# A two-number scaling step of the softmax moved from ScalarE to VectorE, in a kernel whose order a planner lays out

## The chip, the cores and the metric

The kernel runs on one core of a Trainium2 chip. The metric is the device time of one execution, in microseconds, and of several executions the median. A profile is one execution recorded by the hardware profiler. The engines are TensorE (PE; its weight loads are PEld), VectorE (DVE), ScalarE (ACT), GpSimd (POOL) and SyncE (SP), which only issues DMAs here.

## The reference

The input is 16 batches of 512 rows of 512 numbers, f32. Each row is layer-normed once, and the result goes through attention and through a gated feed-forward layer side by side; both results are added to the input.

```python
xn = layernorm(x)                                   # x: 16 x 512 x 512
qkv = xn @ w_qkv.T + b_qkv                          # 16 heads of 32
scores = q @ k.T / sqrt(32) + causal                # 512 x 512 for each head
attn = softmax(scores) @ v
a = attn @ w_out.T + b_out
g = xn @ gate_w.T * gate_s;  u = xn @ up_w.T * up_s # 1408 wide, weights -1, 0, 1
f = (silu(g) * u) @ down_w.T * down_s
out = x + a + f
```

## The kernel before

**Number format.** Values are kept as pairs of f16 (a high part and the rest), so each projection is two or three f16 matmul passes. ScalarE writes the high part, VectorE subtracts it from the f32 value and writes the rest. That is so for the scores' probabilities too (steps `ph` and `pl` below).

**Work.** A batch takes 456 matmuls of 512 columns in the projections (lines 805, 812, 821, 830 and 838), 64 for the scores (line 892) and 192 small ones for attention times values (line 906). TensorE's results go to four PSUM banks `psW`, the scores to four others, `psS`.

**Softmax.** A batch has four groups `G` of four heads. The unit `u` is one head and one block of 128 query rows, so a group has 16 units and the kernel 1024; a unit with block `i` has 128(i+1) keys. Units are joined in 10 cells a group (a block of 512 or the pair 128 and 384 or two of 256, which fills a PSUM bank), so there are 640 cells, 384 of two units and 256 of one. A cell goes through these steps:

- `sn` (PE, line 892): the scores, one matmul a unit, into the cell's `psS` bank
- `max` (DVE, line 1151): adds the mask, finds the row's extreme
- `exp` (ACT, line 1288): exponential in place, with its row sum into `rsum`
- `rc` (DVE, line 1157): `rinv = 1 / rsum`, one instruction for the cell's one or two columns
- `rc2` (ACT, line 1294): `rinv = rinv * 2**14`, in place, one instruction for the cell
- `ph` (ACT, line 1307): `exp * rinv` as f16 into `PL` (or `PL3b`)
- `pl` (DVE, line 1162): the rest as f16
- `pt` (a DMA transpose, line 754): from `PL` to `PT`, when the four heads of a block are done; then `pv` (PE, line 906), `oh` (ACT, 1318), `ol` (DVE, 1166) and the output projection (PE, 821)

A bank of `psS` is free for the next `sn` after the `pl` of the cell four before it.

**Order.** Every engine runs a fixed list of steps. A class `Plan` makes the lists when the kernel is built: it plays the kernel with an assumed duration of each step (`TIMES`) and an assumed delay until another step can use a result (`HOP`, 120 ns for DVE, 130 ns for ACT), and at each moment it gives an engine that is free the ready step with the earliest due time. The due times follow the units, 1795 ns each (`UNIT`); the softmax of the first 160 units is due up to 25 us later (`LATE`), so that it catches up afterwards. At run time the lists are fixed: an engine that has come to a step waits for it, whatever else is ready. A step waits on semaphores that count the finished steps of one kind.

The planner counts `rc` as 100 ns of DVE and `rc2` as 200 ns of ACT, and gives both the same due time:

```python
self.chain(due + 1500, "dve", ("rc", u), ("act", "exp", u))
self.chain(due + 1500, "act", ("rc2", u), ("dve", "rc", u))
```

GpSimd normalises the rows (`nrm`, line 1366), splits them (`xl`, 1375), writes the rest of the hidden values (`hl`, 1383) and adds up the output (`ya` and `yb`, 1388 and 1393). It and VectorE's `tensor_scalar` appear in a list `SHARED` of steps that the planner doesn't let overlap; it names `ffw` (line 1092, VectorE converting the feed-forward weights at the start) but neither `rc` nor `rc2`.

Of the kernel before, what the change touches and what calls it, by code (L numbers as in the profile page):

```python
# [38 lines left out]
    "stats": 605, "aggr": 85, "nrm": 2080, "nrm0": 500, "spread_bv": 1000, "qk_part": 720, "qk_max": 450, "qk_scales": 2100, "qk_small": 650, "wqk_lo": (270, 600),  # L39
    "v_part": 720, "v_max": 100, "v_scales": 1500, "wv_lo": 670, "o_part": 720, "o_max": 100, "o_scales": 1700, "wo_lo": 670, "mid": 550, "xTl": 670, "xTh": 600,  # L40
# [52 lines left out]
class Plan:  # L93
# [254 lines left out]
    def scores(self, u):  # L348
        G = u // 16
        due = AT + UNIT * u - LEAD + self.late(u)  # L350
        c = cell(u)
        units = cell_units(c)
        free = [("dve", "pl", cell_units(c - NS)[-1])] if c >= NS else []
        self.chain(due, "pe", ("sn", u), ("sp", "pk", G), *free)
        self.chain(due + 400, "dve", ("max", u), ("pe", "sn", units[-1]), ("pool", "mask"))
        self.chain(due + 1000, "act", ("exp", u), ("dve", "max", units[-1]))
        if u != units[-1]:
            return
        self.chain(due + 1500, "dve", ("rc", u), ("act", "exp", u))
        self.chain(due + 1500, "act", ("rc2", u), ("dve", "rc", u))  # L360
        for v in units:
            i, h = ORDER[v % 16]
            before = G - 2 if i == 3 else G - 1
            free = [("sp", "pt", before, i)] if before >= 0 else [("pe", "chk", i ^ 1)] * (i >= 2) if G == 0 else [PE_BIAS, ("pe", "chk", 4)]
            self.chain(due + 2000, "act", ("ph", v), ("act", "rc2", u), *free)
        for v in units:
            i, h = ORDER[v % 16]
            self.chain(due + 2600, "dve", ("pl", v), ("act", "ph", u))
            if h == 3:
                free = [("pe", "pv", G - 1)] if G else [("pe", "chk", 12), *(("dve", "wqk_lo", s, 1, 3) for s in range(2)), ("dve", "wv_lo", 1)]  # L370
                self.chain(due + 3000, "sp", ("pt", G, i), ("dve", "pl", v), *free)
# [157 lines left out]
def block_kernel(nc, x, w_qkvT, b_qkv, w_outT, b_out, gateT, upT, downT, gate_s, up_s, down_s, out):  # L529
# [121 lines left out]
    def done(engine, *step):  # L651
        return at[engine, *step]
# [25 lines left out]
    with nc.Block() as block:  # L678
# [278 lines left out]
        def _(e):  # L957
# [41 lines left out]
            for step, *k in plan.order["dve"]:  # L999
# [100 lines left out]
                elif step == "flag2":  # L1100
                    dve.wait_ge(*done("pe", "red", "flag", 1))
                    dve.wait_ge(*done("dve", "ff_scales"))
                    dve.wait_ge(*done("sp", "scale_d"))
                    land(e.tensor_copy(flaga, tile(("red", "flag"))[:, 128:131]))
                    land(e.tensor_scalar(flaga[:, 1:3], flaga[:, 1:3], 0.5, None, op0=ALU.is_lt))
                    e.tensor_reduce(bada, flaga, axis=AX.X, op=ALU.max).then_inc(sem["dve flag2"], 1)
                    dve.wait_ge(*done("dve", "flag2"))
                    land(e.tensor_scalar(okf, bada, 0.0, None, op0=ALU.is_equal))
                    land(e.tensor_tensor(okf, okf, hs[:, 1:2], op=ALU.mult))
                    land(e.tensor_scalar(scale_d[:, :], scale_d[:, :], okf, None, op0=ALU.mult))  # L1110
                elif step == "ql":
                    b, g, which = k
                    bias = bqs[:, 4 * which + g:4 * which + g + 1]
                    dve.wait_ge(*done("act", "qh", b, g, which))
                    e.scalar_tensor_tensor(stg[:, 2 * which + 1, :], tile(("qk", *k))[:, :], bias, stg[:, 2 * which, :], op0=ALU.add, op1=ALU.subtract).then_inc(  # L1115
                        sem["dve ql"], 1)
                elif step == "vl":
                    b, t = k
                    dve.wait_ge(*done("act", "vh", b, t))
                    e.tensor_tensor(V[:, t, 1, :], tile(("v", *k))[:, :], V[:, t, 0, :], op=ALU.subtract).then_inc(sem["dve vl"], 1)  # L1120
                elif step == "yf":
                    b, t = k
                    dve.wait_ge(*done("pe", "o", b, t))
                    dve.wait_ge(*done("pool", "ya", 4 * b + t))
                    e.scalar_tensor_tensor(y[t][:, :], tile(("o", *k))[:, :], s_out, y[t][:, :], op0=ALU.mult, op1=ALU.add).then_inc(sem["dve yf"], 1)
                elif step == "yt":
                    b, t = k
                    dve.wait_ge(*done("pe", "dn", b, t))
                    if b or t:
                        dve.wait_ge(*done("pool", "ya", 4 * b + t - 1))  # L1130
                    else:
                        dve.wait_ge(*done("dve", "flag2"))
                        dve.wait_ge(*done("act", "o_part", 3))
                    e.tensor_tensor(y_t, tile(("dn", *k))[:, :], scale_d[:, :], op=ALU.mult).then_inc(sem["dve yt"], 1)
                elif step == "gate":
                    A = act_t[plan.gu_units[tuple(k)] % 3][:, :]
                    dve.wait_ge(*done("act", "th", *k))
                    e.scalar_tensor_tensor(A, A, 1.0, tile(("ga", *k))[:, :], op0=ALU.add, op1=ALU.mult).then_inc(sem["dve gate"], 1)  # L1138
                elif step == "up":
                    m = k[1]  # L1140
                    A = act_t[plan.gu_units[tuple(k)] % 3][:, :]
                    dve.wait_ge(*done("pe", "up", *k))
                    dve.wait_ge(*done("dve", "gate", *k))
                    dve.wait_ge(*done("dve", "ff_scales"))
                    e.scalar_tensor_tensor(A, tile(("up", *k))[:, :], gus[:, m:m + 1], A, op0=ALU.mult, op1=ALU.mult).then_inc(sem["dve up"], 1)  # L1145
                elif step == "max":
                    u = n
                    s = s_tile(u)
                    dve.wait_ge(*done("pe", "sn", cell_units(cell(u))[-1]))
                    dve.wait_ge(*done("pool", "mask"))  # L1150
                    e.tensor_tensor_reduce(s, s, mask[:, 512 - s.shape[1]:512], scale=negsc, scalar=BIG, op0=ALU.add, op1=ALU.min,  # L1151
                                           accum_out=nmax[:, u % 16:u % 16 + 1]).then_inc(sem["dve max"], 1)
                elif step == "rc":
                    units = cell_units(cell(n))
                    part = slice(units[0] % 16, n % 16 + 1)
                    dve.wait_ge(*done("act", "exp", n))
                    e.reciprocal(rinv[:, part], rsum[:, part]).then_inc(sem["dve rc"], 1)  # L1157
                elif step == "pl":
                    i, h = ORDER[n % 16]
                    out = PLv[pl_tile(n // 16, i)]  # L1160
                    dve.wait_ge(*done("act", "ph", cell_units(cell(n))[-1]))
                    e.scalar_tensor_tensor(out[:, :, 2 * h + 1, :], p_blocks(n), rinv[:, n % 16:n % 16 + 1], out[:, :, 2 * h, :],  # L1162
                                           op0=ALU.mult, op1=ALU.subtract).then_inc(sem["dve pl"], 1)
                elif step == "ol":
                    dve.wait_ge(*done("act", "oh", n))
                    e.scalar_tensor_tensor(oT[:, n % 5, 1, :], tile(("pv", n))[:, :], 2.0 ** -14, oT[:, n % 5, 0, :], op0=ALU.mult, op1=ALU.subtract).then_inc(  # L1166
                        sem["dve ol"], 1)
                else:
                    raise ValueError(step)
# [36 lines left out]
        def _(e):  # L1206
# [9 lines left out]
            for step, *k in plan.order["act"]:  # L1216
# [67 lines left out]
                elif step == "exp":  # L1284
# [2 lines left out]
                    act.wait_ge(*done("dve", "max", cell_units(cell(u))[-1]))  # L1287
                    e.activation(s, s, ACT.Exp, bias=nmax[:, u % 16:u % 16 + 1], scale=-1.0,  # L1288
                                 accum_out=rsum[:, u % 16:u % 16 + 1]).then_inc(sem["act exp"], 1)
                elif step == "rc2":  # L1290
                    units = cell_units(cell(n))
                    part = slice(units[0] % 16, n % 16 + 1)
                    act.wait_ge(*done("dve", "rc", n))
                    e.activation(rinv[:, part], rinv[:, part], ACT.Copy, scale=2.0 ** 14).then_inc(sem["act rc2"], 1)  # L1294
                elif step == "ph":
                    i, h = ORDER[n % 16]
                    before = n // 16 - (2 if i == 3 else 1)
                    act.wait_ge(*done("act", "rc2", cell_units(cell(n))[-1]))
                    if before >= 0:
                        act.wait_ge(*done("sp", "pt", before, i))  # L1300
                    elif n // 16 == 1:
# [140 lines left out]
```

## Time and profile before

| | |
|---|---|
| Time, median of 3 (lowest, highest) | 1911.43 us (1909.62, 1912.43) |
| The profiled execution | 1912.43 us |
| Its span, first to last instruction | 1910.7 us |
| PE busy | 1867.6 us (98%) |
| DVE busy | 1616.4 us (85%) |
| ACT busy | 1471.1 us (77%) |
| POOL busy | 647.7 us (34%) |
| Mean granted TensorE clock | 0.996 |

The span is read from the trace, and 1.7 us of the execution lie around it. A matmul is shown until its result is out, and the next begins before that, so a busy PE is one that isn't seen standing still.

### The profile page before, as it was taken

The page shows a single profiled execution, that of the slowest core. Times are in us where ns is not written, and L with a number is a line of the kernel's source. Part 1 is how long each engine was busy: PE and PEld are TensorE (multiplying, and loading weights), DVE is VectorE, ACT ScalarE, POOL GpSimd, SP SyncE. Part 2 cuts the span into 40 slices and gives each one's busy share as a digit, 9 for nine tenths or more (in the row PEclk, how much of TensorE's full clock was granted, in tenths as well). Part 3 has the DMA queues.
Part 4 walks back from the last instruction along what each step waited for, and adds up shares of the span by engine and source line. Part 5 has one row for each costly group of instructions (what it writes and reads, how often), then busy time and mean ns, then how long its engine had stood idle before and what let it go on. Part 6 is the DMA issues. An engine that isn't in the chain of part 4 may idle for free.

```text
span 1910.7 us, 35064 instructions
## 1 busy us (share of the span) xinstructions
PE 1867.6 (98%) x11560; PEld 879.1 (46%) x11560; DVE 1616.4 (85%) x4697; ACT 1471.1 (77%) x4441; POOL 647.7 (34%) x593
## 2 busy tenths in 40 slices
PE   7899999999999999999999999999999999999997
PEld 3444444444444444444444444444444444444443
DVE  7998999888788888889888788888888888788882
ACT  5678888877787777878877787777878778787771
POOL 1863262342423424233242423424233232312121
PEclk9999999999999999999999999999999999999998
DMA  8399999898988899798997988899798997987893
GB/s 271 82 188 183 173 197 153 162 173 148 163 142 147 153 178 157 143 170 129 173 175 133 172 138 154 156 171 154 151 161 137 178 168 136 156 133 140 131 171 78
DMA packets 805114, 299.90 MB, mean 157 GB/s; under 512 B 734145, under 2 KB 766913, under 8 KB 804929
## 3 DMA queue, kind: packets, MB, share of 16 engines
q1 hardware_dynamic: 804928, 297.62, 88.0%
q8 instruction: 93, 1.52, 0.4%
q14 instruction: 93, 0.75, 0.1%
HBM read 46.94 MB, written 16.78 MB: 33 GB/s over the span
## 4 chain that ended last, share of the span: by engine, by line
PE 79%; DMA 5%; DVE 5%; SPq 4%; POOL 3%; ACT 3%; issue 1%; POOLq 0%; ACTq 0%; DVEq 0%
PE psW L830 28%; PE psW L805 15%; PE psW L838 9%; PE psW L812 8%; PE psW L821 8%; PE psS L892 7%; PE psW L906 5%; DMA PT<-PL 2%; DMA xin<-in_x 2%; SPq L754 2%; DVE PL L1162 1%; SPq L684 1%; DVE psS L1151 1%; POOL xin L1366 1%; ACT PL L1307 1%
## 5 line engine op out<-in xcount | busy, mean ns | idle before, releaser
L830 PE MATMUL psW<-xT,Wgu 128*128 128x512 f16 x2816 | 670.8, 379 | 5.8 <-DVE PT L1115 3.6
L1288 ACT ACTIVATE psS<-psS,small 128x512 f32<-128x512 f32 (+3 forms) x1024 | 516.6, 507 | 163.6 <-DVE small L1151 159.4
L1151 DVE CUSTOM_DVE_ANT_0 psS<-psS,mask,small 128x512 f32<-128x512 f32 (+3 forms) x1024 | 534.5, 551 | 30.3 <-PE psS L892 26.8
L1162 DVE SCALAR_TENSOR_TENSOR PL<-psS,small,PL 128x256 f16<-128x256 f32 (+3 forms) x896 | 424.3, 515 | 54.6 <-ACT PL L1307 53.6
L1383 POOL TENSOR_TENSOR hdn<-act_t,hdn 128x512 f16<-128x512 f32 x176 | 204.3, 1162 | 735.5 <-ACT hdn L1283 735.5
L1307 ACT ACTIVATE PL<-psS,small 128x256 f16<-128x256 f32 (+3 forms) x896 | 400.8, 511 | 19.7 <-DMA PT<-PL 17.5
L830 PEld LDWEIGHTS psW<-xT,Wgu 128*128 128x128 f16 x2816 | 269.8, 97 | 303.0 <-DVE PT L1115 4.1
L805 PE MATMUL psW<-xT,Wqkv 128*128 128x512 f16 x1536 | 363.3, 380 | 0.2 <-DVE act_t L1138 0.2
L838 PE MATMUL psW<-Wdn,hdn 128*128 128x512 f16 x1408 | 316.3, 379 | 0.0
L892 PE MATMUL psS<-QK 96*128 96x512 f16 (+3 forms) x1024 | 252.6, 300 | 12.6 <-DVE PL L1162 10.4
L805 PEld LDWEIGHTS psW<-xT,Wqkv 128*128 128x128 f16 x1536 | 146.1, 98 | 163.2 <-issue 2.2
L1288 ACT ACTIVATION_READ_ACCUMULATOR psS<-psS,small 128x1 f32 x1024 | 217.2, 212 | 0.0
L838 PEld LDWEIGHTS psW<-Wdn,hdn 128*128 128x128 f16 x1408 | 136.7, 98 | 158.7 <-POOL hdn L1383 0.2
L821 PE MATMUL psW<-Wo,oT 128*128 128x512 f16 x768 | 186.9, 382 | 1.5 <-DVE oT L1166 1.5
L812 PE MATMUL psW<-Wqkv,xT 128*128 128x512 f16 x768 | 184.7, 382 | 3.2 <-DVE Wqkv L997 3.2
L1294 ACT ACTIVATE small<-small 128x2 f32<-128x2 f32 (+1 forms) x640 | 124.6, 210 | 52.4 <-DVE small L1157 50.9
L892 PEld LDWEIGHTS psS<-QK 96*128 96x128 f16 x1024 | 95.0, 98 | 142.8 <-DVE PL L1162 41.3
L1283 ACT ACTIVATE hdn<-act_t 128x512 f16<-128x512 f32 x176 | 111.8, 636 | 51.7 <-DVE act_t L1145 51.6
L1275 ACT ACTIVATE act_t<-psW,small 128x512 f32<-128x512 f32 x176 | 121.2, 689 | 32.0 <-PE psW L830 30.2
L1151 DVE DVE_READ_ACCUMULATOR2_ANT small<- 128x1 f32 x1024 | 145.3, 142 | 0.0
L1145 DVE SCALAR_TENSOR_TENSOR act_t<-psW,small,act_t 128x512 f32<-128x512 f32 x176 | 131.2, 745 | 9.5 <-PE psW L830 8.9
L1157 DVE RECIPROCAL small<-small 128x2 f32<-128x2 f32 (+1 forms) x640 | 96.7, 157 | 46.9 <-ACT psS L1288 46.0
(151 smaller groups left out, 1740.6 us busy)
## 6 DMA issues: line engine op xcount, KB each, us to landing
QK<-PT SPq DMA_DIRECT2D x192, 256.0 KB, 5.8
y<-in_x SPq DMA_DIRECT2D x68, 256.0 KB, 3.2
out<-y SPq DMA_DIRECT2D x64, 256.0 KB, 3.5
xin<-in_x SPq DMA_DIRECT2D x60, 256.0 KB, 3.6
PT<-PL SPq DMA_TRANSPOSE x224, 5.1
PT<-in_w_qkvT SPq DMA_DIRECT2D x4, 512.0 KB, 7.1
y<-in_downT SPq DMA_DIRECT2D x4, 256.0 KB, 11.3
xT<-in_w_outT SPq DMA_DIRECT2D x4, 256.0 KB, 3.5
```

The source lines that it names most:

```text
L805: mm = e.matmul(ps[:, :], Wqkv[wl][:, c, c0:c0 + 128], xT[b % 2][:, 4 * xl + c, :], start=(k == 0), stop=last)
L812: mm = e.matmul(ps[:, :], xT[b % 2][:, 4 * xl + c, 128 * t:128 * (t + 1)], Wqkv[wl][:, c, 1024:1536], start=(k == 0), stop=last)
L821: mm = e.matmul(ps[:, :], oT[:, (4 * b + g) % 5, xl, 128 * t:128 * (t + 1)], Wout[wl][:, g, :], start=(k == 0), stop=last)
L830: mm = e.matmul(ps[:, :], Wgu[:, up, c, 128 * m:128 * (m + 1)], xT[b % 2][:, 4 * xl + c, :], start=(k == 0), stop=last)
L838: mm = e.matmul(ps[:, :], hdn[:, m, xl, 128 * t:128 * (t + 1)], Wdn[:, m, :], start=(k == 0), stop=last)
L892: e.matmul(s_tile(u), q[0:96, h, 0, 128 * i:n], q[0:96, h, 1, 0:n], start=True, stop=True).then_inc(sem["pe sn"], 1)
L1145: e.scalar_tensor_tensor(A, tile(("up", *k))[:, :], gus[:, m:m + 1], A, op0=ALU.mult, op1=ALU.mult).then_inc(sem["dve up"], 1)
L1151: e.tensor_tensor_reduce(s, s, mask[:, 512 - s.shape[1]:512], scale=negsc, scalar=BIG, op0=ALU.add, op1=ALU.min, accum_out=nmax[:, u % 16: ...
L1162: e.scalar_tensor_tensor(out[:, :, 2 * h + 1, :], p_blocks(n), rinv[:, n % 16:n % 16 + 1], out[:, :, 2 * h, :], op0=ALU.mult, op1=ALU.subt ...
L1288: e.activation(s, s, ACT.Exp, bias=nmax[:, u % 16:u % 16 + 1], scale=-1.0, accum_out=rsum[:, u % 16:u % 16 + 1]).then_inc(sem["act exp"], 1)
L1307: e.activation(PLv[pl_tile(n // 16, i)][:, :, 2 * h, :], p_blocks(n), ACT.Copy, scale=rinv[:, n % 16:n % 16 + 1]).then_inc(sem["act ph"], 1)
L1383: e.tensor_tensor(hdn[:, m, 1, :], act_t[plan.gu_units[tuple(k)] % 3][:, :], hdn[:, m, 0, :], op=ALU.subtract).then_inc(sem["pool hl"], 1)
```

## The change

The step `rc2` goes from ScalarE's list to VectorE's. There it is a `tensor_scalar` with a constant, in place on the same one or two columns; it waits for `rc`, and `ph` waits for it. The planner gets new durations for both steps, 85 ns each instead of 100 and 200, so it lays out all lists anew.

```diff
-    ... "rc": 100, "rc2": 200, ...
+    ... "rc": 85, "rc2": 85, ...
@@ scores
         self.chain(due + 1500, "dve", ("rc", u), ("act", "exp", u))
-        self.chain(due + 1500, "act", ("rc2", u), ("dve", "rc", u))
+        self.chain(due + 1500, "dve", ("rc2", u), ("dve", "rc", u))
...
-            self.chain(due + 2000, "act", ("ph", v), ("act", "rc2", u), *free)
+            self.chain(due + 2000, "act", ("ph", v), ("dve", "rc2", u), *free)
@@ vector
+                elif step == "rc2":
+                    units = cell_units(cell(n))
+                    part = slice(units[0] % 16, n % 16 + 1)
+                    dve.wait_ge(*done("dve", "rc", n))
+                    e.tensor_scalar(rinv[:, part], rinv[:, part], 2.0 ** 14, None, op0=ALU.mult).then_inc(sem["dve rc2"], 1)
@@ scalar
-                elif step == "rc2":
-                    units = cell_units(cell(n))
-                    part = slice(units[0] % 16, n % 16 + 1)
-                    act.wait_ge(*done("dve", "rc", n))
-                    e.activation(rinv[:, part], rinv[:, part], ACT.Copy, scale=2.0 ** 14).then_inc(sem["act rc2"], 1)
                 elif step == "ph":
...
-                    act.wait_ge(*done("act", "rc2", cell_units(cell(n))[-1]))
+                    act.wait_ge(*done("dve", "rc2", cell_units(cell(n))[-1]))
```

## Rows read from the trace of the kernel before

**Rows 1.** Busy time of each engine by stretch (us, and instructions).

```profile
core 0: us, PE busy (x) PEld busy (x) DVE busy (x) ACT busy (x) POOL busy (x), PEclk, DMA share, GB/s
0.00:60.00 60.00, 44.99 (x197) 21.26 (x198) 48.72 (x123) 32.72 (x79) 20.06 (x32) 0.97 0.72 237
60.00:100.00 40.00, 34.23 (x240) 18.79 (x238) 36.71 (x81) 25.69 (x68) 34.97 (x26) 1.00 0.43 82
100.00:215.00 115.00, 108.38 (x675) 50.00 (x674) 104.84 (x327) 98.09 (x300) 52.82 (x50) 0.99 1.07 180
215.00:330.00 115.00, 114.77 (x756) 54.05 (x754) 106.98 (x330) 99.76 (x312) 46.57 (x44) 1.00 1.00 177
330.00:675.00 345.00, 342.51 (x2126) 160.38 (x2124) 293.33 (x860) 272.81 (x826) 118.82 (x109) 1.00 0.90 156
...
675.00:1710.00 1035.00, 1034.01 (x6412) 487.02 (x6411) 882.03 (x2571) 813.63 (x2465) 333.58 (x301) 1.00 0.91 155
1710.00:1870.00 160.00, 159.17 (x968) 74.70 (x967) 135.62 (x399) 125.50 (x388) 37.11 (x31) 1.00 0.82 144
1870.00:1911.00 41.00, 29.57 (x199) 12.92 (x196) 8.20 (x14) 2.93 (x9) 3.80 (x3) 0.88 0.42 91
```

**Rows 2.** Waits in total, the two small steps and `sn` (us, times, longest).

```profile
ACT small L1294 <- DVE small L1157: 50.9, 97, 2.8
...
PEld psS L892 <- DVE PL L1162: 41.3, 104, 2.8
...
PE psS L892 <- DVE PL L1162: 10.4, 14, 2.5
```

**Rows 3.** The step `rc` (L1157) alone, by stretch: busy, and how many.

```profile
60.00:100.00 40.00, 0.91 (x6) 1.00 0.43 82
100.00:215.00 115.00, 6.93 (x45) 0.99 1.07 180
215.00:330.00 115.00, 6.92 (x46) 1.00 1.00 177
790.00:905.00 115.00, 6.04 (x40) 1.00 0.89 157
```

**Rows 4.** Timeline of VectorE from 25.4 us, one small step behind another.

```profile
25.70 0.17 DVE L973 TENSOR_SCALAR small<-small 128x2 f32<-128x2 f32 x1
25.90 0.16 DVE L1040 TENSOR_TENSOR small<-small 128x2 f32<-128x2 f32 x1
26.09 0.17 DVE L985 TENSOR_SCALAR small<-small 128x2 f32<-128x2 f32 x1
26.30 0.17 DVE L986 RECIPROCAL small<-small 128x2 f32<-128x2 f32 x1
```

**Rows 5.** Timelines of VectorE and of ScalarE from 908 us.

```profile
908.10 0.17 DVE L1157 RECIPROCAL small<-small 128x2 f32<-128x2 f32 x1
908.18 0.74 DVE L1151 CUSTOM_DVE_ANT_0 psS<-psS,mask,small 128x512 f32<-128x512 f32 x1
...
908.96 0.20 ACT L1294 ACTIVATE small<-small 128x2 f32<-128x2 f32 x1
909.05 0.65 ACT L1288 ACTIVATE psS<-psS,small 128x512 f32<-128x512 f32 x1
```

**Rows 6.** Timeline from 112 us, GpSimd and VectorE's `tensor_scalar`.

```profile
112.02 4.15 POOL L1366 TENSOR_SCALAR xin<-xin,small 128x512 f32<-128x512 f32 x2
...
114.77 0.17 DVE L1105 TENSOR_SCALAR small<-small 128x2 f32<-128x2 f32 x1
...
115.55 0.90 DVE L1110 TENSOR_SCALAR scale_d<-scale_d,small 128x512 f32<-128x512 f32 x1
```

**Rows 7.** Timeline from 1870 us, the last cell and the end.

```profile
1871.17 0.16 DVE L1157 RECIPROCAL small<-small 128x2 f32<-128x2 f32 x1
1871.36 0.21 ACT L1294 ACTIVATE small<-small 128x2 f32<-128x2 f32 x1 [0.67 <-DVE small L1157]
1871.60 0.84 ACT L1307 ACTIVATE PL<-psS,small 128x384 f16<-128x384 f32 x2
...
1888.33 3.39 PE L906 MATMUL psW<-PT,V 128*32 128x512 f16 x48 [4.80 <-DMA PT<-PL]
```

2 rows, old and new, of the table TIMES are left out of this document.

## The prediction

> **What bounds the kernel now.** I read the busy time by stretch first, then the waits, then timelines of the places where the two small steps stand.
>
> TensorE is the bound. From 675 to 1710 us it is busy 1034.0 of 1035 us, at full clock, while DVE is busy 882.0 (85%) and ACT 813.6 (79%) [rows 1]. Nothing that makes DVE or ACT a little faster or slower there can be seen in the end, as long as both stay below TensorE and no result comes later than TensorE's list asks for it. TensorE stands still visibly in few places, read as stretch minus busy in [rows 1]: 15.0 us before 60 us (loads and weight scales, before softmax is of any size), 5.8 from 60 to 100, 6.6 from 100 to 215, 0.2 from 215 to 330, 2.5 from 330 to 675, 1.0 to 1710, 0.8 to 1870, and 11.4 in the tail.
>
> The second thing to see is that DVE is nearly full early on. The softmax starts late and catches up: `rc` is run 45 and 46 times in the two stretches of 115 us from 100 to 330 us, against 40 in such a stretch later [rows 3]. DVE is busy 104.8 and 107.0 of 115 us in them, ACT 98.1 and 99.8 [rows 1]. So the change moves work from the second fullest to the fullest of the two helpers, just where there is least room.
>
> The third is how softmax stops TensorE: `sn` waits for the `pl` that frees its bank, 10.4 us in all on the matmul, and 41.3 us on its weight load, most of which lies under the matmul before it [rows 2]. So the latency of a cell counts a little.
>
> **What comes off ACT.** 640 instructions. In a stream, the instruction behind `rc2` begins 0.09 us after it (908.96 to 909.05 in [rows 5]), so 640 x 0.09 = 58 us of ACT's time come free, and up to 640 x 0.20 = 128 us where nothing is behind it (0.20 us is its own duration). ACT also stood idle 50.9 us ahead of `rc2`, waiting for `rc` [rows 2]; that wait passes to `ph`, which now waits for DVE in the same way. All of it lies beside TensorE's work: 0 us.
>
> **What goes onto DVE.** The trace has a `tensor_scalar` of 128x2 f32 on the same small tile: 0.17 us [rows 4]. If another instruction stands between it and `rc`, it costs what `rc` costs in a stream: the next begins 0.08 us later (908.10 to 908.18, [rows 5]). If it stands right behind `rc` and waits for its result, the pair is like the chain of dependent small steps in [rows 4], which begin 0.19 to 0.21 us apart, so `rc2` adds 0.20 us. Hence 640 x 0.08 = 51 us to 640 x 0.20 = 128 us more DVE in all. By stage:
>
> - 675 to 1710 us: nine stretches of 40 cells, 360 x 0.08 to 0.20 = 29 to 72 us on 882, so 911 to 954 of 1035. It fits under TensorE, with at least 81 us to spare: 0 us.
> - 100 to 330 us: 91 cells, 7 to 18 us on 211.8, so 219 to 230 of 230. It fits barely, or only just not.
> - 60 to 100 us has 6 cells, about 1 us more in 3.3 us idle.
>
> **Latency of a cell.** The shortest way from `rc` to `ph` is to be seen at the last cell: `rc` begins at 1871.17, `rc2` at 1871.36, `ph` at 1871.60, so 0.43 us [rows 7]. After the change it is 0.20 (to `rc2`, rows 4) + 0.17 (its duration) + 0.03 (the hop to the other engine, taken from the end of `rc` at 1871.33 to 1871.36, [rows 7]) = 0.40 us. Where ACT is occupied, the difference is larger: at 908 us `rc` began at 908.10 and `rc2` only at 908.96, since ACT was at work on an `exp` [rows 5]. On DVE it would have come after 0.20 us, or behind the `max` that followed, about 0.7 us. So a busy cell wins 0.1 to 0.6 us. What is queued behind the new instruction on DVE (`max`, `pl`, and the evacuations of `psW`, for which TensorE waits) loses 0.08 to 0.20 us for each. I take the two as equal: between 100 and 330 us, where both matter, the cells' gain makes the banks free sooner and the load makes DVE later.
>
> A rule of the Trainium skill speaks against this change, and is weighed here because rows bear on it. The row first: a `tensor_scalar` of 512 columns begun at 115.55 took 0.90 us, ending 0.28 us after GpSimd's instruction, which ran until 116.17; the one of 2 columns, begun at 114.77 while the same GpSimd work was running, took 0.17 us as it does elsewhere [rows 4, 6]. The Trainium skill (SBUF — State Buffer, "Who interferes with whom") says that a VectorE instruction in a mode with two ports and a GpSimd instruction exclude one another for the whole instruction; and VectorE: DVE Perf Modes ("What auto-detection actually checks") has the mode taken by an SBUF-to-SBUF `tensor_scalar` with an even count, which `rc2` is in 384 of 640 cases. The long instruction agrees with it, the short one doesn't. By the row the term is 0; by the rule it is the fourth case below.
>
> **The rest of the plan.** The lists are laid out anew on all engines, with ACT counted 200 ns less a cell and DVE 85 + 85 - 100 = 70 ns more. That shuffles the order everywhere. Its price can't be read; its bounds can. No order can win more than the idle time of TensorE that softmax can touch: 6.6 + 0.2 + 2.5 + 1.0 + 0.8 us from 100 to 1870 us and the 4.8 us for which the last `pv` waits for transposes [rows 7], 15.9 us in all. For the loss, the nearest row is the stretch from 330 to 675: 2.5 us in 345 instead of 1.0 in 1035, which over the 1035 us would be 7.5 - 1.0 = 6.5 us more. I take 0, since both counted durations are near the measured steps (0.085 beside 0.08, and 0.085 + 0.120 for the pair beside 0.20).
>
> **The tail.** After the last `ph` come transposes, `pv`, and the output projection; none changes. The last cells have 0.43 against 0.40 us: 0 us within what can be read.
>
> **Sum.** 1912.4 (the profiled execution; its span 1910.7 + 1.7) + 0 (ACT) + 0 (DVE under TensorE) + 0 (start, two terms against one another) + 0 (order) = 1912.4 us. That execution was the slowest of three; the median is 1.0 us less, so I forecast 1911.4, say 1911.
>
> **The rivals.**
>
> 1. *Nothing to be seen* (forecast): TensorE's load stays the bound, DVE's additional work goes into its idle time. For: 99.9% busy from 675 to 1710 us. Against: the start has little room. 1911 us.
> 2. *Faster through shorter cells.* ACT, relieved of a step, starts `exp` and `ph` sooner, banks come free sooner, and TensorE's stops at `sn` shrink. For: 97 waits of ACT at `rc2`, and 10.4 us of stops at `sn` [rows 2]. Against: the wait only moves to `ph`. Half of the 15.9 us: 1903 to 1904 us.
> 3. *Slower: DVE becomes the bound during the catch-up.* Place: 100 to 330 us. DVE's 18.2 us idle there are waits for results that don't vanish when more work is put in, so its work stretches the stage by what is added, 7 to 18 us; TensorE can fill part of it with feed-forward work, so I take the lower end. It decides from the point where DVE's additional work there exceeds what its idle time absorbs, that is, if most `rc2` stand right behind their `rc` (0.20, not 0.08). 1911 + 7 = 1918 us.
> 4. *Slower through GpSimd.* If `rc2` waited for GpSimd after all: GpSimd is busy 33% of the time (333.6 of 1035), one of its instructions lasts some 1.2 to 2.1 us, so a step meets one in a third of cases and waits about 0.6 us, 0.2 us on the mean. In the catch-up 91 x (0.20 + 0.20) = 36 us on 18 idle, at least 18 us late: 1930 us. Against it stands the row of 0.17 us.
> 5. *The step doesn't get cheaper in latency*: the planner, which lets 120 ns pass after `rc`, fits a long DVE instruction (0.75 us) between the two each time. Then cells are as long as before, DVE pays only 0.08, and the time is that of case 1.
>
> **How the numbers follow.** Chances: case 1 with 5, 0.44; case 2, 0.29; case 3 with an unlucky order, 0.23; case 4, 0.04. Changes under 0.2% (3.8 us) can't be told from none. Faster 0.29, same 0.44, slower 0.27. The range goes to the middle of case 2 and past case 3, 1903 to 1921, and leaves out a better order than half of the idle time, and case 4. Case 1 alone is 1908 to 1915.
>
> **What would show it.** L1294 gone from ACT, 640 `tensor_scalar` of 0.15 to 0.17 us on DVE; one of 0.5 us or more is case 4. DVE busy 50 to 128 us more, ACT 60 to 128 less. PE busy from 675 to 1710 us as before. PE's idle time from 100 to 330 us: 6.8 us now, less in case 2, above 12 in case 3. In case 2 the waits of `sn` for `pl` fall below 10.4 us. The prediction is wrong if TensorE's stops, spread in the middle of the run, turn out to depend on the order laid out anew more than on any engine's load.

## The result and the profile after

The changed kernel takes 1930.9 us (median of 4, 1929.1 to 1932.7) against 1910.9 us before (4, 1909.6 to 1912.4): a ratio of 1.0102, 95% interval 1.0087 to 1.0117. It is 20 us slower. The forecast was 1911 us and no change; the measured time lies outside the range as well.

The profiled execution has a span of 1930.4 us. First the busy time of each engine by stretch, as in [rows 1]:

```profile
0.00:60.00 60.00, 42.99 (x178) 19.86 (x179) 47.95 (x125) 31.26 (x73) 18.81 (x31) 0.91 0.72 237
60.00:100.00 40.00, 34.76 (x246) 19.16 (x245) 36.99 (x84) 24.40 (x61) 33.25 (x26) 1.00 0.39 78
100.00:215.00 115.00, 102.05 (x634) 46.12 (x633) 110.79 (x353) 88.92 (x244) 50.26 (x46) 0.97 0.97 169
215.00:330.00 115.00, 114.12 (x712) 53.46 (x711) 107.49 (x355) 90.47 (x250) 43.01 (x40) 1.00 1.00 177
330.00:675.00 345.00, 340.93 (x2114) 158.81 (x2113) 309.78 (x980) 256.76 (x699) 123.95 (x115) 1.00 0.90 158
675.00:1710.00 1035.00, 1029.26 (x6382) 482.75 (x6380) 921.45 (x2914) 766.91 (x2097) 335.03 (x302) 1.00 0.90 154
1710.00:1870.00 160.00, 158.94 (x1004) 74.24 (x1003) 140.71 (x448) 117.69 (x325) 31.38 (x27) 1.00 0.78 136
```

ScalarE (ACT) has less to do and VectorE (DVE) more, as the change says. From 100 to 215 us DVE is busy 110.8 of 115 us and TensorE stands still 13.0 us instead of 6.6; from 675 to 1710 us TensorE stands still 5.7 us instead of 1.0. The new instruction by its two widths (busy, mean ns of one), among the groups of instructions:

```profile
L1162 DVE TENSOR_SCALAR small<-small 128x2 f32<-128x2 f32 x384 | 99.1, 259 | 4.2
L1162 DVE TENSOR_SCALAR small<-small 128x1 f32<-128x1 f32 x256 | 36.6, 147 | 3.4
```

With one column it takes what was forecast, 0.15 us. With two it takes 0.26 us on the mean, not 0.17. Two places in the timeline show why:

```profile
351.39 2.08 POOL L1366 TENSOR_SCALAR xin<-xin,small 128x512 f32<-128x512 f32 x1
351.55 0.62 DVE L1162 TENSOR_SCALAR small<-small 128x2 f32<-128x2 f32 x1
...
1146.62 1.16 POOL L1383 TENSOR_TENSOR hdn<-act_t,hdn 128x512 f16<-128x512 f32 x1 [8.49 <-ACT hdn L1288]
1146.77 1.09 DVE L1162 TENSOR_SCALAR small<-small 128x2 f32<-128x2 f32 x2
...
1147.84 1.42 ACT L1307 ACTIVATE PL<-psS,small 128x384 f16<-128x384 f32 x3 [0.63 <-DVE small L1162]
```

At 1146.62 us GpSimd begins a step of 1.16 us; `rc2` begins 0.15 us later on DVE and is over only when GpSimd is (the row joins it with the next one), and ScalarE stands idle 0.63 us for it. Counted over the trace, 74 of the 384 two-column `rc2` last over 0.25 us, all of them begun during a GpSimd instruction. Of these, 63 end 21 to 26 ns after that instruction, and the other 11 at the same point within it, 0.78 us after its start, as in the first two rows. None of the 256 one-column ones is long, though 79 begin during GpSimd's work. What the two-column ones take above 0.16 us adds up to 38 us.

Where the time went can be read from the last matmul of the down projection (line 838) of the second, the ninth and the last batch. The last start in each stretch stands behind the "to", before and then after:

```profile
L838 PE MATMUL psW<-Wdn,hdn x176: 377/379/389, 113.7 to 281.7; 128*128 128x512 f16 x176
L838 PE MATMUL psW<-Wdn,hdn x792: 377/379/389, 113.7 to 1089.8; 128*128 128x512 f16 x198
L838 PE MATMUL psW<-Wdn,hdn x1408: 377/379/390, 113.7 to 1883.1; 128*128 128x512 f16 x176
```

```profile
L838 PE MATMUL psW<-Wdn,hdn x176: 376/379/382, 116.3 to 293.5; 128*128 128x512 f16 x176
L838 PE MATMUL psW<-Wdn,hdn x792: 376/379/382, 116.3 to 1104.3; 128*128 128x512 f16 x198
L838 PE MATMUL psW<-Wdn,hdn x1408: 376/379/390, 116.3 to 1905.5; 128*128 128x512 f16 x176
```

So 11.8 us are lost by the end of the second batch, 2.7 in the next seven, 7.9 in the last seven, and the tail after it is 2.7 us shorter (24.9 us instead of 27.6; the granted clock in it is 0.93 instead of 0.81).

### The profile page after: what moved, and what is told of

Read it like the earlier page. It is cut to its first block, busy times and chain, and to the rows that moved or that the text cites. A ratio compares the mean times of both kernels' runs of the same rounds, so it can differ in the third digit from the quotient of the medians.

```text
span 1930.4 us, 35063 instructions
## 1 busy us (share of the span) xinstructions
PE 1872.0 (97%) x11560; PEld 876.3 (45%) x11560; DVE 1705.7 (88%) x5337; ACT 1397.9 (72%) x3801; POOL 647.4 (34%) x593
## 4 chain that ended last, share of the span: by engine, by line
PE 63%; DVE 17%; DMA 8%; SPq 4%; ACT 3%; issue 3%; POOL 2%; ACTq 0%; POOLq 0%; DVEq 0%
PE psW L830 21%; PE psW L805 13%; PE psW L812 8%; PE psW L821 7%; PE psW L838 6%; PE psS L892 5%; DVE PL L1167 4%; PE psW L906 4%; DVE psS L1151 4%; DMA PT<-PL 4%; DMA xin<-in_x 3%; SPq L754 2%; ACT PL L1307 1%; DVE act_t L1145 1%; DVE PL3b L1167 1%
## 5 line engine op out<-in xcount | busy, mean ns | idle before, releaser
L1167 DVE SCALAR_TENSOR_TENSOR PL<-psS,small,PL 128x256 f16<-128x256 f32 (+3 forms) x896 | 418.7, 513 | 55.2 <-ACT PL L1307 54.4
L1307 ACT ACTIVATE PL<-psS,small 128x256 f16<-128x256 f32 (+3 forms) x896 | 394.8, 512 | 74.5 <-DVE small L1162 45.1
L1293 ACT ACTIVATION_READ_ACCUMULATOR psS<-psS,small 128x1 f32 x1024 | 221.1, 216 | 0.0
L1162 DVE TENSOR_SCALAR small<-small 128x2 f32<-128x2 f32 (+1 forms) x640 | 134.1, 214 | 7.7
L1138 DVE SCALAR_TENSOR_TENSOR act_t<-act_t,psW 128x512 f32<-128x512 f32 x176 | 119.4, 679 | 15.6 <-ACT act_t L1280 15.6
```

Source lines behind the costliest of these rows:

```text
L1307: e.activation(PLv[pl_tile(n // 16, i)][:, :, 2 * h, :], p_blocks(n), ACT.Copy, scale=rinv[:, n % 16:n % 16 + 1]).then_inc(sem["act ph"], 1)
```

## The experiments

Three theories stood at the start. **L**: GpSimd holds the two-column `rc2`. **D**: the load that `rc2` puts on VectorE costs the time. **O**, later **S**: the lists that the planner lays out anew are worse, whatever is in them. In the table "lists" says whose order the engines run; the last columns are the start of the last down matmul of batch 2 and of batch 16 in the profile (281.7 and 1883.1 before). The medians come from several chips, so the ratio, to the kernel before on the same chip, is what compares. A profile is one execution: those of e9 and e10 took 1917.7 and 1927.2 us, some 5 us more than their medians, so their last two columns are late by a part of that.

| run | lists | rc2 | median us | ratio (95%) | batch 2 | batch 16 |
|---|---|---|---|---|---|---|
| after | new | DVE | 1930.9 | 1.0102 (1.0087-1.0117) | 293.5 | 1905.5 |
| e1 | new | DVE, one column | 1926.5 | 1.0083 (1.0064-1.0102) | 289.4 | 1897.6 |
| e13 | new | left out | 1920.7 | 1.0059 (1.0042-1.0076) | 286.8 | 1893.3 |
| e12 | before | left out | 1909.6 | 1.0000 (0.9991-1.0010) | 281.6 | 1882.7 |
| e4 | before | ACT, spare on DVE | 1913.2 | 1.0017 (1.0007-1.0027) | 283.0 | 1886.5 |
| e3 | before | ACT, wide spare | 1934.3 | 1.0125 (1.0100-1.0149) | 288.2 | 1907.7 |
| e14 | before | DVE, apart from rc | 1925.4 | 1.0089 (1.0073-1.0106) | 283.2 | 1895.5 |
| e6 | before | DVE, one column | 1942.1 | 1.0165 (1.0147-1.0183) | 292.5 | 1913.1 |
| e5 | before | DVE | 1969.7 | 1.0307 (1.0283-1.0331) | 295.4 | 1940.5 |
| e15 | before | ACT, waiting spare | 1969.5 | 1.0317 (1.0300-1.0334) | 299.7 | 1942.1 |
| e8 | rc 95, rc2 200 | ACT | 1910.9 | 1.0005 (0.9995-1.0014) | 282.1 | 1884.4 |
| e9 | rc 100, rc2 150 | ACT | 1913.0 | 1.0016 (1.0005-1.0028) | 284.5 | 1889.4 |
| e2 | rc 85, rc2 85 | ACT | 1922.4 | 1.0066 (1.0047-1.0086) | 289.7 | 1894.7 |
| e10 | rc 80, rc2 80 | DVE, one column | 1921.8 | 1.0063 (1.0047-1.0080) | 288.7 | 1897.5 |
| e7 | rc 100, rc2 200 | DVE | 1934.7 | 1.0126 (1.0106-1.0146) | 307.7 | 1914.4 |

**e1: GpSimd can't hold it, the changed kernel's lists.**

```diff
-e.tensor_scalar(rinv[:, part], rinv[:, part], 2.0 ** 14, None, op0=ALU.mult).then_inc(sem["dve rc2"], 1)
+for c in range(part.start, part.stop):
+    ins = e.tensor_scalar(rinv[:, c:c + 1], rinv[:, c:c + 1], 2.0 ** 14, None, op0=ALU.mult)
+ins.then_inc(sem["dve rc2"], 1)
```

> The changed kernel with the same order on every engine; only, where rc2 covers two columns it is two tensor_scalar of one column each. In the changed kernel 74 of the 384 two-column rc2 last 0.66 us on the mean and none of the 256 one-column ones is long. Theory L (GpSimd holds the two-column ones, and the 38 us of VectorE time lost so cost most of the 20 us): no long rc2, time 1911 to 1919. Theory D (VectorE's additional load costs it): 384 more instructions, 31 us more load, so 1931 or more. Theory O (the order laid out anew is the worse one): 1926 to 1932.

The instruction is short again (1024 of them, 0.147 us on the mean), but only about 4 of the 20 us come back: 1.0083 instead of 1.0102, with intervals that overlap. The spans say 6.4 us (1924.0 against 1930.4). The time is what O expected (1926 to 1932). L by itself was wrong, and so was the size that I gave it.

**e2: the planner's numbers alone.** `rc2` stays on ScalarE:

```diff
-"rc": 100, "rc2": 200,
+"rc": 85, "rc2": 85,
```

> The kernel before, rc2 still on ScalarE, with the changed kernel's durations in the planner (85 and 85). Theory O, in the form that the planner's numbers alone make a worse order: 1920 or more. Theories L and D: 1908 to 1914, as before.

1.0066: lists laid out with other numbers lose 12.6 us with the same work on the same engines. That speaks for O.

**e3 and e4: a spare instruction on the lists of before.** Behind each `rc`, reading a constant; `cols` is the cell's width in e3 and 1 in e4:

```diff
 e.reciprocal(rinv[:, part], rsum[:, part]).then_inc(sem["dve rc"], 1)
+cols = part.stop - part.start
+dve.wait_ge("dve pad", pads[0])
+pads[0] += 1
+e.tensor_scalar(spare[:, 0:cols], cs[:, 0:cols], 2.0 ** 14, None, op0=ALU.mult).then_inc(sem["dve pad"], 1)
```

> The kernel before with its own order, and behind every rc one more tensor_scalar on VectorE of the width of rc (one or two columns), from a constant to a scratch column, that nothing waits for and the planner doesn't know; rc2 stays on ScalarE. Theory L: some 75 of the 384 wide ones are long, 1918 to 1930. Theory D: 1918 to 1930 too, but then e4 is as slow. Theory O: within 4 us of before.

> As e3, with one column always. Same number of instructions (640), none that GpSimd can hold. Theory L: 1910 to 1914. Theory D: the same time as e3, 1918 to 1930. Theory O: within 4 us of before.

The groups of instructions of e3, and then of e4:

```profile
L1161 DVE TENSOR_SCALAR small<-small 128x2 f32<-128x2 f32 x384 | 96.0, 250 | 0.0
L1161 DVE TENSOR_SCALAR small<-small 128x1 f32<-128x1 f32 x256 | 35.1, 137 | 0.0
```

```profile
L1161 DVE TENSOR_SCALAR small<-small 128x1 f32<-128x1 f32 x640 | 86.5, 135 | 0.0
```

The only difference is the second column of 384 instructions, and it makes 21 us (1934.3, above the 1918 to 1930 that was expected, against 1913.2). In e3, 62 are long, 38 us in all, as many us as in the changed kernel. So the hold is dear where the lists know nothing of it. 640 more instructions that nobody holds cost 3 us.

**e5 and e6: the move alone.** The lists are those of before; ScalarE has nothing to do at the place of `rc2`, and VectorE runs it directly behind `rc` (e6 with one column at a time):

```diff
 e.reciprocal(rinv[:, part], rsum[:, part]).then_inc(sem["dve rc"], 1)
+dve.wait_ge(*done("dve", "rc", n))
+e.tensor_scalar(rinv[:, part], rinv[:, part], 2.0 ** 14, None, op0=ALU.mult).then_inc(sem["act rc2"], 1)
...
-act.wait_ge(*done("dve", "rc", n))
-e.activation(rinv[:, part], rinv[:, part], ACT.Copy, scale=2.0 ** 14).then_inc(sem["act rc2"], 1)
+pass
```

> The move alone, on the lists of the kernel before: the planner still counts rc2 on ScalarE with 200 ns, ScalarE does nothing at that place, and VectorE runs rc2 directly behind its rc, with the wait on rc, one or two columns wide as in the changed kernel. Theory L (GpSimd holds the two-column ones): 60 to 75 long ones, 1928 to 1936. Theory O (the loss is from the lists laid out anew): within 5 us of before. Theory D (load of VectorE, 0.20 us a pair): as e6.

> As e5, but two tensor_scalar of one column each where the cell has two. Theory L: no long one, 1911 to 1918, and the difference to e5 is about the 21 us by which the wide spare instruction was slower than the narrow one. Theory D: 1925 or more.

They cost 59 and 32 us, far more than theory L expected of either; e6 is what D expected. The hold is confirmed a second time (28 us between them, and 93 long ones in e5), but e6, where nothing is held, costs nine times what e4 does (32 against 3.4 us). The timeline of e4, and then of e6, on VectorE:

```profile
909.58 0.17 DVE L1157 RECIPROCAL small<-small 128x2 f32<-128x2 f32 x1
909.66 0.14 DVE L1161 TENSOR_SCALAR small<-small 128x1 f32<-128x1 f32 x1
909.71 0.75 DVE L1151 CUSTOM_DVE_ANT_0 psS<-psS,mask,small 128x512 f32<-128x512 f32 x1
```

```profile
908.16 0.17 DVE L1157 RECIPROCAL small<-small 128x2 f32<-128x2 f32 x1
908.36 0.21 DVE L1160 TENSOR_SCALAR small<-small 128x1 f32<-128x1 f32 x2
908.50 0.35 DVE L1151 CUSTOM_DVE_ANT_0 psS<-psS,mask,small 128x128 f32<-128x128 f32 x1
```

In e4 the step behind `rc` begins 0.13 us after it; in e6, 0.34 us after it, because `rc2` waits for the result of `rc` and then has two columns to do one by one.

**e7: the old numbers for the new place.** The changed kernel with `"rc": 100, "rc2": 200`.

> The changed kernel, rc2 on VectorE, but the planner counts 100 ns for rc and 200 for rc2. If the planner's short durations are what hurts (no room in the lists for a step that is held), this is 5 us or more faster than the changed kernel, 1915 to 1926. If the lists only happen to be good or bad, it lies anywhere from 1920 to 1940.

1.0126: not faster, though the planner leaves more room. Most of the loss is in the first two batches: the last down matmul of batch 2 starts at 307.7 us, 26 us later than before, and the remaining fourteen batches lose only 5.3 us more, against 10.6 in the changed kernel (1905.5 - 1883.1 less 11.8), although `rc2` is held in this kernel too (0.272 us on the mean with two columns). That suggests that the lists of the start are one matter and the room in the rest another; one pair of lists doesn't show it. A part of the 26 us is the clock: from 100 to 215 us TensorE stands still 19.5 us, and the granted clock is 0.89, against 0.99 before, which is worth at most 11 us there.

**e8 and e9: other numbers for the old place.** The kernel before with `"rc": 95, "rc2": 200` and with `"rc": 100, "rc2": 150`.

> The kernel before, rc2 on ScalarE, planner's rc 95 ns instead of 100: a change without meaning for the work. If the lists of before are a lucky draw, and any change of a number loses some of it, 1916 to 1926, near the kernel with 85 and 85. If those two numbers as such are what is wrong, 1908 to 1914.

> The kernel before, rc2 on ScalarE, planner's rc2 150 ns instead of 200. Theory R (reserve: the 200 counted for a step that takes 94 ns in a stream leaves ScalarE time in the lists, and without it the lists are too tight): between before and the kernel with 85 and 85 (1922), so 1914 to 1919. Theory S (the lists are a draw, mainly of the first two batches): anything from 1908 to 1924, with the difference already there by 290 us.

Five nanoseconds on `rc` change nothing that can be told (1.0005). Fifty on `rc2` cost 3 us, with 85 and 85 it is 12.6. So not every change of a number does harm. But e8 is a weak trial of that: counted over the traces, with the small scaling steps left out, 89% of VectorE's instructions stand in e8 at the same place of the order as before, 59% in e9, 54% in the changed kernel and 46% in e2. The lists of e8 are nearly those of before, and no lists that differ much were as fast. Between R and S in the expectation of e9 these runs don't decide, since 3 us is less than R asked for, and has the sign of both.

**e10: other lists for the new place.** e1 with `"rc": 80, "rc2": 80`.

> The changed kernel with one-column rc2 (as e1), planner's numbers 80 and 80 instead of 85 and 85: another draw of lists with rc2 on VectorE that GpSimd can't hold. Theory S: 1911 to 1930, unlike e1's 1926. Theory D (VectorE's load in the catch-up costs what e1 costs, whatever the list): 1923 to 1930.

1.0063 against 1.0083 of e1, intervals overlapping: another draw of lists is not clearly another time. Its 1921.8 us lie within what S expected and 1.2 us under what D did.

**e12: rc2 taken off ScalarE and put nowhere**, on the lists of before; `rc` sets the semaphore that `ph` waits for.

> The lists of the kernel before, rc2 left out on every engine (the factor 2**14 is missing from the probabilities, so the attention output is too small by it); ph waits for rc. It shows what taking the step off ScalarE is worth by itself. All theories of the prediction: TensorE is the bound, so 1905 to 1911; if shorter cells matter (case 2 of the prediction), 1903 to 1905.

1.0000 (0.9991 at the least), with ScalarE busy 1398.4 us instead of 1471.1. This is the top of what any way of moving the step off ScalarE can bring on these lists: nothing that can be told.

**e13: the changed kernel's lists with rc2 left out.**

```diff
-e.reciprocal(rinv[:, part], rsum[:, part]).then_inc(sem["dve rc"], 1)
+e.reciprocal(rinv[:, part], rsum[:, part]).then_inc(sem["dve rc2"], 1)
...
-dve.wait_ge(*done("dve", "rc", n))
-e.tensor_scalar(rinv[:, part], rinv[:, part], 2.0 ** 14, None, op0=ALU.mult).then_inc(sem["dve rc2"], 1)
+pass
```

> The changed kernel's lists on every engine, rc2 left out (the factor 2**14 is missing from the probabilities, so the attention output is too small by it), ph waits for rc. Theory S (the new lists are worse by themselves): 1920 to 1925, as the lists of 85 and 85 with rc2 on ScalarE. Theory D (VectorE's load costs the 16 us of e1): 1908 to 1913.

1.0059: 11 to 12 of the 20 us are there although neither engine runs `rc2`. The last starts of the down matmuls, to be read as above:

```profile
L838 PE MATMUL psW<-Wdn,hdn x176: 376/379/389, 117.3 to 286.8; 128*128 128x512 f16 x176
L838 PE MATMUL psW<-Wdn,hdn x792: 376/379/389, 117.3 to 1096.0; 128*128 128x512 f16 x198
L838 PE MATMUL psW<-Wdn,hdn x1408: 376/379/390, 117.3 to 1893.3; 128*128 128x512 f16 x176
```

5.1 us are lost by batch 2, 1.1 in the next seven, 4.0 in the last seven. In the later part TensorE stops at `sn` for a bank. The waits of TensorE from 675 to 1710 us, before, after and in e13:

```profile
PE psS L892 <- DVE PL L1162: 0.7, 1, 0.7
```

```profile
PE psS L892 <- DVE PL L1167: 5.3, 7, 0.9
```

```profile
PE psS L892 <- DVE PL L1166: 4.8, 10, 0.9
```

One place of the list repeats with the batches. In e13, from 1440 us:

```profile
1444.65 0.63 ACT L1228 ACTIVATE xhl<-xin 128x512 f16<-128x512 f32 x1 [1.94 <-POOL xin L1365]
1445.19 2.71 ACT L1306 ACTIVATE PL<-psS,small 128x256 f16<-128x256 f32 x6
...
1446.05 2.19 DVE L1166 SCALAR_TENSOR_TENSOR PL<-psS,small,PL 128x256 f16<-128x256 f32 x4 [1.86 <-ACT PL L1306]
...
1446.98 0.39 PE L892 MATMUL psS<-QK 96*128 96x384 f16 x2 [0.71 <-DVE PL L1166]
```

Read upwards: `sn` waits for a `pl`, which waits for a `ph`, and the `ph` stand on ScalarE behind the high part of a row block (L1228), which waits 1.94 us for GpSimd's normalisation. Six of the ten stops in e13 have this form, one a batch, and so have five of the seven in the changed kernel (the one at 1457 us is 0.88 us) and five in e2 (at 1449 us 0.86 us, behind a shorter wait for GpSimd of 0.98 us); nearly all others, as that at 1424 us in the changed kernel, stand behind a `ph` that waits for a transpose to free its `PL`. ScalarE's wait for GpSimd is no news of the new lists. In e12, on the lists of before, it is there too:

```profile
1434.48 0.63 ACT L1224 ACTIVATE xhl<-xin 128x512 f16<-128x512 f32 x1 [1.68 <-POOL xin L1365]
...
1437.75 0.38 PE L892 MATMUL psS<-QK 96*128 96x384 f16 x2
```

There TensorE comes to the `sn` 3.3 us after that step of ScalarE began and doesn't wait; in e13 it comes 1.6 us after (1446.98 less the stop of 0.71). So at this place the new lists ask for the same result sooner than it can be there.

**e14: rc2 in the chain, but not right behind its rc.** As e6, with one other VectorE step between where that step is neither a `pl` nor an `rc`.

> The lists of before, rc2 on VectorE in one-column instructions, as e6, but one other step of VectorE stands between rc and rc2 wherever that step is neither a pl nor another rc. If the 192 ns stand of rc2 behind its own rc costs the 32 us of e6, this gives back what its share of the cells is, 1920 to 1932; if rc2 coming later makes the cells longer and that decides, 1942 or more.

1.0089 instead of 1.0165: half of e6's cost comes back with the same instructions, although `rc2` comes later for its cell. On the lists of before, too, work added on VectorE brings up the stop that e13 has once a batch: counted over the traces from 675 to 1710 us, six times in e14 (0.6 to 1.0 us each) and eight times in e3 (0.3 to 1.8 us), behind the same wait of ScalarE for GpSimd. In the kernel before no stop there has it.

**e15: the stand without the chain.** As e4, but one or two one-column spare instructions, which wait for `rc`; nothing waits for them.

> The kernel before, rc2 on ScalarE, and behind every rc one or two spare one-column tensor_scalar on VectorE that wait for rc as in e6 but that nothing waits for. VectorE is occupied as in e6. Theory D (occupation of VectorE, stands included): 1935 to 1942. If it is the longer way to ph instead: 1911 to 1917.

```profile
911.02 0.16 DVE L1157 RECIPROCAL small<-small 128x2 f32<-128x2 f32 x1
911.29 0.21 DVE L1162 TENSOR_SCALAR small<-small 128x1 f32<-128x1 f32 x2
911.42 0.75 DVE L1151 CUSTOM_DVE_ANT_0 psS<-psS,mask,small 128x512 f32<-128x512 f32 x1
```

It is no match for e6 as meant: with two waits before it, the spare instruction begins 0.27 us after `rc` (911.02 to 911.29), not 0.20. It costs 60 us, beyond what either theory expected, without touching the way from `exp` to `ph`. So VectorE's time beyond what the planner counted is dear by itself. How much of e6's 32 us is the longer way from `rc` to `ph` was not told apart. In the busy time and instructions of each engine, e4 and then e6:

```profile
PE 1867.7 (98%) x11560; PEld 874.7 (46%) x11560; DVE 1646.3 (86%) x5337; ACT 1472.8 (77%) x4441; POOL 648.5 (34%) x593
```

```profile
PE 1882.7 (97%) x11560; PEld 872.8 (45%) x11560; DVE 1722.6 (89%) x5721; ACT 1405.4 (73%) x3801; POOL 648.0 (33%) x593
```

VectorE's busy time above before (1616.4 us) is 30 us in e4, 66 in e14, 106 in e6 and 104 in e15. Idle time right before the added instructions comes to it: 7 us in e14, 23 in e6 and 70 in e15. The spans are longer by 2, 12, 28 and 58 us. So the first 30 us are nearly free, and each one after that costs a quarter to two thirds of itself, on lists that have no room for it; e3 fits, with 68 us more and a span longer by 23.

## Why the prediction was wrong

**The sum.** Of the 20 us, the lists laid out anew are 11 to 12 (e13, 1.0059), `rc2` on VectorE some 4 or 5 (1.0083 of e1 less 1.0059), the hold by GpSimd some 4 (1.0102 less 1.0083). The last two are uncertain by about 5 us each, from the intervals, as much as they are themselves, and e1 issues 384 instructions more than the changed kernel, so that the hold is rather more and the load rather less. Shown by their intervals are the first and the sum of the other two (1.0102 less 1.0059, 8 us, uncertain by about 4); that the hold and the load each cost time is shown on the lists of before (e3 against e4, e5 against e6, e6 against e12), where they cost more. The split holds for the new lists only. On the lists of before the same move costs 59 us (e5): the new lists lose 11 to 12 us by themselves, and yet spare 39 of these.

**What bounds the kernel** was read rightly: TensorE is busy 99.4% from 675 to 1710 us after, too. The conclusion drawn from it was wrong: that nothing beside it can be seen "as long as both stay below TensorE". e15 leaves VectorE 13% idle (busy 1720.5 of 1968.3 us) and costs 3%. The second half of the same sentence, "and no result comes later than TensorE's list asks for it", was the one that mattered, and I costed it at nothing.

**What comes off ACT**: 0 us, right, and shown (e12). ACT's busy time fell by 73 us, within the forecast's 58 to 128 us. Case 2, faster through shorter cells with 0.29, had nothing behind it.

**What goes onto DVE**: the pieces were sized right. A one-column `rc2` takes 0.15 us; the pair with its wait steps 0.20 us, a stream 0.08 or less. Busy time rose by 89 us, within 51 to 128. The steps "it fits under TensorE: 0 us" and "I take the two as equal" failed: there is no such exchange between shorter cells and VectorE's load, because shorter cells are worth nothing (e12) and load beyond the lists' count is dear (e6, e14, e15).

**The rule against the change** was weighed wrongly, and this is the step with the plainest lesson. One row of 0.17 us was set against a rule. In [rows 6] GpSimd's L1366 runs twice, the second time from 114.09 us (4.15 us for two, 2.08 each), and L1105 began 0.68 us after that and ended 0.85 us after it. The changed kernel has 28 two-column `rc2` begun during L1366: the eleven begun in its first 0.5 us end 0.78 us after its start (one stands above, 351.39 to 352.17), none of the six begun between 0.70 and 1.27 us is long, and one begun at 1.73 us ends with it; the other ten begin in its last 0.17 us. So the row came from the gap in which this GpSimd instruction holds nothing, and said nothing about the rule. The size given to case 4 was 0.2 us on the mean for each of the 640; measured is 38 us over the 384 with two columns, 0.10 us each, and 0 for one column. Its chance of 0.04 was too low; its time, 1930 us, was near, but for a reason that makes up a fifth of it.

**The rest of the plan**: this is the term that failed most, and the last sign in the prediction's own list, that TensorE's stops might depend on the order more than on any engine's load, is what came. It was bounded at +6.5 us, from a row of the kernel before, and taken as 0 "since both counted durations are near the measured steps". Measured: 11 to 12 us. Numbers near the truth are no promise of as good a list. e2 has them too and loses 12.6 us. The bound came from the wrong place: half of the loss falls before 290 us, a stretch to which I gave no loss from the order at all. What the bound didn't see is how close behind ScalarE and VectorE the new lists let TensorE ask (the rows under e13).

**Case 3**, DVE as the bound in the catch-up, has its place right: from 100 to 330 us TensorE stood idle 13.8 us (above the 12 named as the sign), DVE was busy 218.3 of 230 us, and 11.8 us are lost by the end of batch 2. But e13 loses 5.1 of them, with TensorE idle 11.2 us and VectorE busy 211.7 us in these stretches, as before; so less than 7 us of it can be the load and the hold, and the sign was nearly met by the order alone.

**The tail**: 0 was forecast, on a way of 0.40 us. The last cell of the changed kernel:

```profile
1893.52 0.17 DVE L1157 RECIPROCAL small<-small 128x2 f32<-128x2 f32 x1
1893.72 0.17 DVE L1162 TENSOR_SCALAR small<-small 128x2 f32<-128x2 f32 x1
1893.93 0.84 ACT L1307 ACTIVATE PL<-psS,small 128x384 f16<-128x384 f32 x2 [0.44 <-DVE small L1162]
```

0.41 us, as worked out.

**The clock** is no explanation of the changed kernel's loss. The granted clock from 0 to 60 us is 0.91 after and 0.97 before, but it is 0.91 there in e8 and e12 too, which lose nothing. From 100 to 215 us it is 0.97 and 0.99, at most some 2 us, with a TensorE that stood still 13.0 us instead of 6.6. Only in e7 is it a large part.

**What stays open.** Why the lists of before are better than those with 85 and 85 isn't settled. The late part is mostly one stop of `sn` a batch, where TensorE's list asks sooner than before for what ScalarE gives only after a wait for GpSimd; why the planner puts it there wasn't followed, and the early part wasn't followed to a single place. Whether the 200 ns counted for `rc2` is a reserve that is missed, or the lists of before are a fortunate draw, was not told apart by e7 to e10. No version faster than the kernel before was found, and e12 says that on its lists there is none to be had from this step.

## What to carry to other kernels

A change of an engine's work in a kernel whose order is laid out by a planner is two changes. Run the new order with the old work, and the new work on the old order, before reading anything into the sum; here the order was more than half. An engine that is 10 to 15% idle next to the bound has no free time if its instructions run in a fixed list: what counts is how late each result is against the place where the list asks for it, so small unplanned instructions that wait for the one before them cost many times what the same ones cost without the wait (60 us in e15, 3 in e4). And a single row that contradicts a rule should be looked at for when it ran, not only for how long.

## What the runs showed of the hardware

The unexpected point is how the hold depends on width and on time. A `tensor_scalar` of f32 in SBUF with two columns begun during a GpSimd instruction of 512 columns is as a rule held until that is over, and ends 21 to 28 ns after (74 of 384 are long in the changed kernel, 62 in e3, 93 in e5). The nine begun during GpSimd's one-column `tensor_tensor` (L1362, 0.56 us) in the changed kernel weren't held (0.15 us). With one column it was held in none of 256 cases in the changed kernel and none of 640 in e4; in e1 one of 1024 took 0.34 us, right behind a 3x3 `tensor_scalar` that was itself long (0.48 us). No `rc`, a reciprocal of one or two columns, was held either (0.170 us at most before). The Trainium skill (VectorE: DVE Perf Modes, "What auto-detection actually checks") has the mode with two ports depend on the outermost dimension being even or equal in source and destination; the two-column case agrees, and the one-column case shows that a single column doesn't take it. The Trainium skill (SBUF — State Buffer, "SBUF: two separate sides") says that the pair of ports is held for the whole instruction. Here GpSimd's `tensor_scalar` of 128x512 (2.08 us) let two-column instructions pass between 0.7 and 1.3 us after its start and held those begun 0.14 to 0.5 us and 1.5 to 1.9 us after it (the changed kernel, e3 and e7), so for this one the trace differs. Nine begun 0.10 to 0.14 us after it in e3 passed too.

Also, a small VectorE step that waits for the one right before it begins 0.19 to 0.20 us after it (e6), where an independent one begins 0.08 us after (e4), and with two waits in front 0.27 us (e15).
